# Unread bf16 products in TensorE's waits of the stand-alone routing and ahead of the first attention's norm

## What is computed

```python
x = x + 0.5 * _L0_ffn_ref(_layernorm(x, axis=-1), ...)   # experts, call 0
x = x + _L0_attn_ref(_layernorm(x, axis=-1), ...)        # attention, 16 heads
x = x + 0.5 * _L0_ffn_ref(_layernorm(x, axis=-1), ...)   # experts, call 1
# inside the experts' block, for one batch of tokens
scores = jax.nn.softmax(xf @ gate_w.T, axis=-1)
topk_w, topk_idx = jax.lax.top_k(scores, K)              # K = 6 of 64 experts
# each token's row is put in a slot of each chosen expert (64 slots each), by its rank there
hid = jax.nn.silu(g) * u; eo = einsum(hid, down_proj) * buf_w
shared = silu(xf @ shared_gate_w.T) * (xf @ shared_up_w.T) @ shared_down_w.T
```

## Time and profile before

| | us |
|---|---|
| runs | 787.88, 789.38, 783.97 |
| median | 787.88 |
| the profiled execution's time | 787.34 |
| its span in the profile | 785.7 |
| busy: TensorE products / weight loads | 577.7 / 368.9 |
| busy: VectorE / GpSimd / ScalarE | 389.2 / 295.2 / 233.4 |
| mean granted TensorE clock | 0.85 of full speed |

### The profile page before, as it was taken

The page is one execution under the profiler, slowest core; times in us unless marked ns, Lnnn a source line. Parts: engine busy times, 40 slices in busy tenths (PEclk is TensorE's granted clock), DMA queues, the critical chain, the costliest instruction groups (busy, mean ns, idle before and its releaser), DMA issues. The chain is left out here.

```text
span 785.7 us, 10359 instructions
## 1 busy us (share of the span) xinstructions
PE 577.7 (74%) x3486; PEld 368.9 (47%) x3486; DVE 389.2 (50%) x1102; ACT 233.4 (30%) x638; POOL 295.2 (38%) x383
## 2 busy tenths in 40 slices
PE   2666259970799999998953398984336697897796
PEld 1334125530466666665632254564213586554485
DVE  4656213333475676855442033366758547624135
ACT  1222024440132232321310144420033463142664
POOL 0556611106601537160326012257754266003065
PEclk9757569995799999998985599987577798998899
DMA  8886048842200314340166168733370000000001
GB/s 322 290 295 215 16 129 271 282 164 80 73 9 1 81 41 85 35 170 4 37 241 138 55 211 301 243 104 98 89 80 1 0 1 1 1 1 0 2 1 53
DMA packets 39723, 82.96 MB, mean 106 GB/s; under 512 B 7805, under 2 KB 27906, under 8 KB 38816
## 3 DMA queue, kind: packets, MB, share of 16 engines
q1 hardware_dynamic: 26144, 45.03, 17.7%
q0 software_dynamic: 13248, 37.07, 17.2%
q10 hardware_dynamic: 288, 0.30, 0.1%
HBM read 60.21 MB, written 26.35 MB: 110 GB/s over the span
## 5 line engine op out<-in xcount | busy, mean ns | idle before, releaser
L434 POOL DMA_INDIRECT expert_in<-xn_sent,scatter_slots x72 | 70.9, 985 | 79.7 <-DVE slots L383 50.5
L770 DVE SCALAR_TENSOR_TENSOR work<-work,banks 128x96 f32<-128x96 f32 x64 | 16.3, 254 | 124.1 <-ACT work L750 124.1
L1845 PE MATMUL banks<-w_gu,w_dn 128*128 128x256 f32 x256 | 68.4, 394 | 0.0
L1610 POOL DMA_INDIRECT w_dn<-expert_out,slots x48 | 51.3, 1069 | 26.4 <-issue 14.2
L790 PE MATMUL banks<-ident,work 128*128 128x128 f32 x128 | 29.5, 316 | 42.6 <-DMA work<-expert_in 42.6
L1251 POOL DMA_INDIRECT w_gu<-expert_out,gather_slots x48 | 49.3, 1028 | 28.7 <-DVE gather_slots L1259 14.7
L799 PE MATMUL banks<-w_gu,work 128*64 128x192 f32 x512 | 58.5, 352 | 0.0
L1968 POOL TENSOR_TENSOR var_eps<-mv,eps 128x1 f32<-128x1 f32 (+1 forms) x70 | 13.7, 195 | 116.8 <-ACT w_dn L1894 55.2
L1845 PEld LDWEIGHTS banks<-w_gu,w_dn 128*128 128x128 f32 x256 | 46.0, 199 | 4.2
L790 PEld LDWEIGHTS banks<-ident,work 128*128 128x128 f32 x128 | 13.8, 149 | 67.5 <-issue 41.5
L1970 POOL TENSOR_TENSOR rstd<-var_eps,minus_half 128x1 f32<-128x1 f32 (+1 forms) x70 | 42.4, 606 | 5.5
(11 more groups left out here) (271 smaller groups left out, 1258.0 us busy)
## 6 DMA issues: line engine op xcount, KB each, us to landing
work<-expert_in SPq DMA_DIRECT2D x64, 128.0 KB, 3.8
expert_out<-work SPq DMA_DIRECT2D x64, 128.0 KB, 3.8
w_gu<-in_gate_up SPq DMA_DIRECT2D x10, 768.0 KB
w_gu<-in_gate_up POOLq DMA_DIRECT2D x6, 768.0 KB, 5.6
expert_in<-w_dn SPq DMA_DIRECT2D x4, 1024.0 KB, 7.5
w_dn<-in_down SPq DMA_DIRECT2D x10, 384.0 KB
w_gu<-in_gate_up SPq DMA_DIRECT2D x1, 3840.0 KB, 12.0
w_dn<-in_down SPq DMA_DIRECT2D x1, 3072.0 KB, 25.8
```

Of the source, the lines that this page charges most:

```text
L434: nc.gpsimd.indirect_dma_start(out=m.expert_in, out_offset=bass.IndirectOffsetOnAxis(m.scatter_slots[u][:, at:at + 1], 0), in_=xn[:, t, :] ...
L1610: nc.gpsimd.indirect_dma_start(out=w.combined[q % 2][:, t * TOPK + k, :], out_offset=None, in_=m.expert_out, in_offset=bass.IndirectOffset ...
L1845: last = nc.tensor.matmul(f.p_lin[t % DEEP], f.uT[t % DEEP][:, c, :], w.lin[:, step, c, :], start=(step > 0 and c == 0), stop=(c == KC - 1))
```

## The change

`keep_busy` gets the bank as a parameter. `route_tensor` now issues 4 unread products ahead of the logits, 14 ahead of the rank products, and 4 ahead of the shared expert's output product, all into bank 5, which routing alone leaves free. In the middle phase TensorE first waits for the second tile's gathered rows, then issues 16 unread products, then goes on to the norm's transposition. After the last attention it issues 14 before the last norm's transposition. That is 5 x 22 + 30 = 140 more products. No other engine's list changes.

```diff
@@ route_tensor
+    keep_busy(nc, m, 4, FREE_BANK)
     route_tensor_logits(nc, m, r, eng, s, ready)
     route_tensor_shared(nc, m, r, s, 0)
+    keep_busy(nc, m, 14, FREE_BANK)
     route_tensor_rank(nc, m, r, eng, s, turn)
     route_tensor_shared(nc, m, r, s, 1)
     route_tensor_hidden(nc, m, r, eng, s, turn)
     if then:
         then()
+    keep_busy(nc, m, 4, FREE_BANK)
     route_tensor_out(nc, m, r, eng, s, turn)
@@
-def keep_busy(nc, m, n):
+def keep_busy(nc, m, n, bank=2):
     for _ in range(n):
-        nc.tensor.matmul(m.banks[:, 2, 0:3 * P], m.ident_b[:, 0:P], m.causal_b[:, :], start=True, stop=True)
+        nc.tensor.matmul(m.banks[:, bank, 0:3 * P], m.ident_b[:, 0:P], m.causal_b[:, :], start=True, stop=True)
@@ middle_phase, tensor
+            pe.wait_ge(comb.gathered[TB - 1], 16 * TOPK)
+            keep_busy(nc, m, 16)
             for step in range(3):
                 ahead(0, step)
             turn(0, first=True)
             with pe.Fori(1, B - 1) as i:
                 turn(i)
             turn(B - 1, is_last=True)
+            keep_busy(nc, m, 14)
             norm_tensor(nc, m, pe, norm, 2 * B - 1, m.xn_sent, p_norm)
             route_tensor(nc, m, r, pe, sr, (norm.xnT, 2 * B), 2 * B - 1)
```

More of the change, by code:

```diff
@@ L198, in __init__ @@
         self.rank_read = sem(f"{name}_rank_read")
+FREE_BANK = 5
 class RoutePlaces:
```

## The result

The changed kernel takes 781.79 us (median of 16 runs, 778.87 to 786.31), the kernel before 787.13 on the same chip (16 runs). The ratio is 0.9951, 95% interval 0.9928 to 0.9974: 2.0 to 5.7 us faster, and still within 1%. The time lies inside the range; the forecast of a gain of 1.7 us was too small, less than half of the 3.9 us that the ratio gives.

What follows compares the result with a forecast made beforehand. It took GpSimd's scatters and their landing to bound the first phase, TensorE and VectorE in series the middle phase's start, and slots the last scatter. From 787.34, + 1.9 - 2.7 - 0.9 = - 1.7 gave 785.6 us, range 780.5 to 791.

Steps and rivals of the forecast that it cites:

- rival 1: First phase hides everything because its unread products raise the clock there too; 3.6 us less, 783.7; chance 0.20.
- The price of one product: One unread product on TensorE costs 0.17 us at full clock and 0.30 at half clock.
- First phase, turn 0 (+ 1.5): First routing turn: four and fourteen products outlast their waits, 1.5 us later (bounds 1.1 and 2.9), first scatter about 28.
- First phase, turns 1 to 3 (+ 2.8 each): Later routing turns: two fours at half clock and the fourteen lengthen each by 2.8 us (1.4 to 4.6).
- The slack: First phase: idle 2.77 and 0.77 us before two norms, and last slots 4.4 us before the last scatter, absorb delay.
- Its landing ... has time to lose: First phase: the first scatter's 1.5 us delay was left out, its landing being held by other transfers.
- Sum of the first phase (+ 1.9): Whole first phase: last slots at 86.1, 1.9 us after the old last scatter; ends 0 and + 8.7.
- Start of the middle phase (- 2.7): Sixteen products ahead of the norm bring full clock; the q/k/v records take 5.6 instead of 8.37 us.
- rival 2: Middle phase: the clock does not hold to the q/k/v products; 1.0 us more, 788.3; chance 0.15.
- Last routing (- 0.9): After the last attention the clock stays up; router product 1.10 instead of 1.97 us, last scatter 0.9 earlier.
- The sum: Whole kernel: + 1.9 - 2.7 - 0.9 = - 1.7 us, from 787.34 to 785.6.
- A stage that the change does not touch moves by more than 2 us: Any untouched stage: a move of over 2 us was named as a sign that the prediction is wrong.

Runs made afterwards that it cites:

- e8_thirty_six_last: Changed kernel with 36 instead of 20 unread products in the last attention's wait for its normed tile; 779.8 us, ratio to before 0.9914.
- e5_fourteens_only: Changed kernel without both groups of four in each routing turn; 783.9 us, ratio to before 0.9965.
- e2_first_phase_only: Kernel before plus only the 4, 14 and 4 in the first phase's four turns; 785.8 us, ratio to before 0.9992.
- e10_no_first_36: As e8_thirty_six_last, but with no unread products in the first phase; 784.9 us, ratio to before 0.9952.
- e13_warm_no_first: As e12, but without the first phase's unread products; 780.1 us, ratio to before 0.9886.
- e7_twenty_eight: Changed kernel with 28 instead of 14 unread products ahead of the rank in the first phase's turns; 782.6 us, ratio to before 0.9951.
- e12: As e8_thirty_six_last, plus unread products in the waits at the last attention's end and ahead of both expert calls; 778.8 us, ratio to before 0.9870.
- e4_all_again: The changed kernel itself, run once more beside kernels with its single parts; 782.4 us, ratio to before 0.9958.
- e6_sixteen_unanchored: Changed kernel without the wait on the last gathered rows ahead of the sixteen, so they execute earlier; 784.4 us, ratio to before 0.9964.

## Why the prediction was right, and where it was not

The time came out in the range because the range took in rival 1 (783.7, a gain of 3.6), to which the prediction gave 0.20. The forecast's own course, a first phase that gets 1.9 us longer, did not come true. That the number was right is in part luck.

**The price of one product** held at full clock and was a little low at half: four at full clock 0.81, fourteen 2.44, sixteen begun at half clock 4.14, against 0.7, 2.4 and "at most 4.8". The row behind the 0.30 at half clock was misread. In the kernel before, the window from 675.00 to 675.50 has a granted clock of 0.78, so the clock rose before those twelve ended. In the changed kernel four at a granted 0.50 take 1.28 us from start to start (29.79 to 31.07), 0.32 each. From fourteen (2.44) to thirty-six (6.01, e8_thirty_six_last) at full clock the length grows by 3.57, 0.162 each. The estimates by the Trainium skill ("TensorE: Matmul & The Clock Gate", Back-to-back issue gap), 0.32 and 0.16 us, agree with both.

**First phase, turn 0 (+ 1.5).** Measured + 0.2 in the changed profile. Over the seven kernels with 4, 14, 4 the first scatter starts at 26.4 to 27.0 six times and once at 28.34 (mean 26.9); over the five with no products in the first phase at 26.4 to 26.9 (mean 26.6). The bounds of the step held only for that one. Its reading of the clock was off: I took the row of before, where the clock rises about when the fourteen would start. With the four ahead of it, it mostly rises inside the shared product, which takes 1.70 in the changed kernel and 1.51 to 2.87 (mean 2.1) in the eight kernels with the fours, against 2.55 to 2.87 (mean 2.8) in the six without. e5_fourteens_only, without the fours, is at 28.24, close to the step's "at about 28", and so is e2_first_phase_only, with them, at 28.34.

**First phase, turns 1 to 3 (+ 2.8 each).** This step failed. It charged two blocks of four at half clock and gave nothing back. The output product fell from 3.65 to 2.33, the router product from 1.81 to 1.00, the shared product from 2.63 to 1.51, and the fourteen went at full clock. In turn 1 all eight kernels with the fours have 1.00 and 1.51 there. They make the early rise likely but are not its only cause: of the six without the fours, e10_no_first_36 and e13_warm_no_first have 1.00 and 1.51 as well, the other four 1.81 and 2.6 to 2.9. Rival 1 said this, with 0.20 of the chance and - 3.6; its argument against ("two dense-looking stretches at 0.50 for 6 us now") was read from a row that itself had no answer to what denser work would do.

**The slack.** That turns have time to spare was right, and more so than I reckoned: e7_twenty_eight shows that a turn even hides twenty-eight.

**"Its landing ... has time to lose".** Mostly wrong. A late first scatter passes on: 28.34 gave 106.60 and 28.24 gave 106.88 for the start of call 0, against 104.0 to 105.5 in the other kernels with fourteen or none. Of e7_twenty_eight's 2.5 us, 0.7 were absorbed in the landing. (From first to second scatter it takes 21.0 us there and 21.7 to 23.1 in the other kernels, so this figure is no better than about 1 us.) The omission cost the forecast nothing only because turn 0 was hardly late.

**Sum of the first phase (+ 1.9).** Call 0 begins at 105.2 on average with the products (seven kernels), at 104.7 without (five): + 0.5. By this mark they bring nothing. The whole times do not settle it: with the products the ratio is lower in all three pairs, by 0.6 us (e2_first_phase_only against before, 1.6 either way), 3.0 (e8 against e10, 3.2) and 1.3 (e12 against e13, over 4). None is clear of its uncertainty, and no row shows where such a gain would come from. Whether the products can be left out without loss is open by 1 to 3 us.

**Start of the middle phase (- 2.7).** Right in kind, and all but right in size. The clock was 1.00 when the q/k/v products started, their 16 records took 5.43 (forecast 5.6), and the stage fell by 3.4, since transposition and rotary waits shortened as well. But it does not always happen: of ten kernels with the sixteen in place six have 12.65, four 14.2 to 14.4. In these four the clock rose as well, and fell back when the q/k/v products had just begun, as rival 2 had it in part. In e4_all_again the norm's transposition took 0.76 us after a pause of 1.05, so still at full clock; the granted clock is 1.00 from 201.0 to 201.5, 0.68 in the half microsecond after it and 0.50 then:

```profile
194.38 4.66 PE L937 MATMUL banks<-causal_b,ident_b 128*128 128x384 bf16 x16 [21.30 <-DMA w_gu<-expert_out,gather_slots]
...
200.08 0.76 PE L172 MATMUL banks<-ident,xn 128*128 128x128 f32 x4 [1.05 <-DVE xn L151]
201.52 7.12 PE L928 MATMUL banks<-w_qkv,w_gu 128*128 128x512 f32 x16 [0.68 <-ACT w_gu L179]
...
203.00:205.00 2.00, 2.00 (x4) 0.71 (x3) 0.00 (x0) 0.00 (x0) 1.61 (x2) 0.50 0.47 129
```

The length of the pause does not decide it. In the six that kept the clock the sixteen took 4.06 to 4.41 us, so the clock came up earlier within them, and the pause behind was the longer one (1.30 to 1.65 us). In the four that lost it they took 4.50 to 4.66, and the pause was 1.05 to 1.22. Whether more than sixteen would keep the clock each time was not tried.

The mean of the ten is 13.3, that of the three without the sixteen 15.4: - 2.1. "No row excludes that" the gain is lost was the right caution; its share should have gone into the term.

**Last routing (- 0.9).** Right: - 0.98, router product 1.11 (forecast 1.10), and eleven kernels with the fourteen agree to within 0.02 us.

**The sum.** With the measured terms it is + 0.5 - 2.1 - 1.0 = - 2.6 instead of - 1.7, against the measured - 3.9 (2.0 to 5.7) and, repeated, - 3.3 (1.9 to 4.7). Both intervals take in the - 2.6, so nothing more need be missing. The mis-sized term is the first phase's, + 1.9 for what measured + 0.5.

**"A stage that the change does not touch moves by more than 2 us".** Call 1 went from 74.20 to 71.53, and the last attention hardly at all. By my own words that makes the prediction wrong. What the fourteen profiles show is that the sign was ill chosen: call 1 lies between 70.9 and 76.1 us and the last attention, where its products are twenty, between 53.3 and 57.0, with no order by what was changed that I can see. The profiled execution of after is one with a short call 1.

## What to carry to other kernels

Unread products pay where a wait ends in front of work on the path and nothing else on that path is late: they must stand directly ahead of it, and long enough to bridge the wait. Where another engine paces the loop (here GpSimd's scatter and its landing) they are free, and the loop gets no faster by them; find that out first, by the distance between two turns. And when the forecast adds work beside a slow clock, price the work behind it at both levels: what comes back can be more than what was added.

## What the runs showed of the hardware

- The clock's rise and fall do not repeat between kernels that are alike up to that place. In turn 0 of the first phase the shared product took between 1.51 and 2.87 us behind the same instructions in eight kernels; the first scatter lies at 26.38 behind one of the shortest and at 28.34 behind the longest. A term that hangs on one such edge should be a mixture of its two levels.
- A wait is not harmless because it was so in one profile. Behind the same waits of 0.81, 1.43 and 0.67 us at the last attention's end the projection took 1.99 us in the changed kernel and 3.78 in e4_all_again, which is the same kernel. With products in these waits it took 1.99 or 2.00 in all three kernels that have them.
- Sixteen products that end 20 us before the work lift the clock and lose it again: 1.00 from 182 to 185, 0.50 from 187 to 200 (e6_sixteen_unanchored).
- GpSimd's bare raise of a semaphore stood behind its tenth scatter issue in its list, and TensorE was let go by it at 417.02 or before, while the fifth of twelve issues (416.04 to 417.02) was under way; the tenth began at 422.46. So it does not mark that the issues ahead of it have been made.
- Waits for rows in call 1 vary from 0.15 to 4.7 us with the same code (but for ten products at the start of the call in the last two kernels), with 297 to 361 GB/s moved in the window from 464 to 482. They are one of the largest differences between the profiles, beside the clock.
